# Per-subject residual matmul: the first trip round the ring of x is loaded by SP, and each store waits for a later load

## The chip, the cores and the metric

One core of one Trainium2 chip. The metric is the device time of one execution in microseconds (us). The kernel before takes 327.24 us, the median of three runs (326.29 to 327.82). All rows below are of one profiled execution, which took 326.55 us with a span of 324.0 us.

## The reference

For each of 128 samples, a [128, 1024] block of f32 is multiplied by the 128 x 128 weight matrix of its subject and added to itself:

```
w = weights[subjects]                        # weights [8, 128, 128], subjects [128]
out = x + einsum('bct,bcd->bdt', x, w)       # x, out [128, 128, 1024] f32
```

x is 64 MiB and out is 64 MiB.

## The kernel before, in words

The residual costs no pass of its own: an identity is added to the weights, so that one matmul gives x + x*w. A *tile* is two samples, a *pair* is two tiles (four samples, 2 MiB of x and 2 MiB of out). There are 64 tiles, 32 pairs.

- **Loads of x.** `x_ring` has 10 slots for tiles, that is 5 places for pairs. One DMA loads one pair, in pieces of 8 KB. GpSimd (POOL) issues all 32 loads (L133), so they all run on queue q0. It issues pairs 0 to 3 at the start, then before each further load it copies the pair's four weight matrices out of `weight_bank` into `weight_ring` (L150). Pair p from 5 on waits until TensorE has multiplied pair p - 5, which frees its place. Each of the 5 places has a semaphore `x_in`, which a load raises by 16, one from each DMA engine. Pair 4 waits for the landing of pair 0.
- **Matmuls (PE, L235).** 16 weight loads and 16 matmuls for a tile, into one of two PSUM products. The loop `Fori(0, LAPS)` runs 6 laps of 10 tiles, and 4 tiles are written out behind it. Six warm-up matmuls stand ahead.
- **Copies out of PSUM.** A tile has 8 blocks of 32 x 1024; ACT copies 4 or 5 of them (L221), DVE the rest (L199), into `results`, a ring of 6 pairs.
- **Stores.** SP issues one DMA for a pair, in pieces of 16 KB, on queue q1, where the load of the weights (L103) was the first. Ahead of the store of pair p it waits for the copies of pair p and then, at L112, for the landing of pair p + 4 (`X_FIRST`). Stores 28 to 31 have no such wait. The copies of pair p wait for the store of pair p - 6.

The order of work is thus set by the order of instructions on each engine and by semaphores; there is no planner. Each DMA of x or out runs on all 16 DMA engines; a DMA engine that has work on both queues shares its time between them.

Of the kernel before, what the change touches and what calls it, by code (L numbers as in the profile page):

```python
# [6 lines left out]
DMA_INC = 16  # L7
SLOTS = 10
PAIR = 2
LOADS_AHEAD = 4  # L10
PRODUCTS = 2
RESULTS = 6
WARM_UP = 6
X_FIRST = 4


def subject_residual_kernel(nc, x, subjects, weights, out):
# [11 lines left out]
    f32, i32 = mybir.dt.float32, mybir.dt.int32  # L29
    B, C, T = x.shape  # L30
    S, _, D = weights.shape
    assert C == D == nc.NUM_PARTITIONS
    R, Q = 2, 4
    H, K = C // R, D // Q
    TILES = B // 2
    LAPS, REST = divmod(TILES, SLOTS)
    assert LAPS and SLOTS % PRODUCTS == 0 and REST % PRODUCTS == 0
    PAIRS, PAIR_SLOTS = TILES // PAIR, SLOTS // PAIR
    assert SLOTS % PAIR == 0 and REST % PAIR == 0 and LOADS_AHEAD == X_FIRST == PAIR_SLOTS - 1 and PAIR * 2 * K == C
    BANKS = T // PSUM_BANK_COLS  # L40

    SUBJECT_ROWS = 16
# [8 lines left out]
    x_of_pair = x.rearrange("(n j a) (h r) t -> n (a h) j (r t)", j=PAIR, a=2, r=R)  # L51
    out_of_pair = out.rearrange("(n g) (k q) t -> n (g k) (q t)", g=PAIR * 2, q=Q)

    with ExitStack() as ctx:  # L54
        x_ring = ctx.enter_context(nc.sbuf_tensor("x_ring", [C, SLOTS, R, T], f32))
# [19 lines left out]
        bank_low = ctx.enter_context(nc.semaphore("bank_low"))  # L75
        bank_high = ctx.enter_context(nc.semaphore("bank_high"))

        x_in = [ctx.enter_context(nc.semaphore(f"x_in{s}")) for s in range(PAIR_SLOTS)]

        pair_out = [ctx.enter_context(nc.semaphore(f"pair_out{s}")) for s in range(RESULTS)]  # L80
# [20 lines left out]
        @block.sync  # L101
        def _(sp):
            sp.dma_start(weight_halves[:, :, :, :],  # L103
                         weights.rearrange("(i a) (h r) d -> (a h) i (r d)", a=2, r=R)).then_inc(weights_in, DMA_INC)
            for pair in range(PAIRS):
                place = pair % RESULTS
                sp.wait_ge(act_copied, (pair + 1) * PAIR + PRODUCTS)
                sp.wait_ge(dve_copied, (pair + 1) * PAIR + PRODUCTS)

                ahead = pair + X_FIRST  # L110
                if ahead < PAIRS:
                    sp.wait_ge(x_in[ahead % PAIR_SLOTS], (ahead // PAIR_SLOTS + 1) * DMA_INC)  # L112
                sp.dma_start(out_of_pair[pair], results[:, place, :, :]).then_inc(pair_out[place], DMA_INC)
            for place in range(RESULTS):
                sp.wait_ge(pair_out[place], DMA_INC * len(range(place, PAIRS, RESULTS)))

        @block.gpsimd
        def _(pool):
            def subjects_of(pair):

                _, numbers = nc.values_load_multi_w_load_instructions(
                    subject_row[0:1, pair * PAIR * 2:(pair + 2) * PAIR * 2], engines=(mybir.EngineType.Pool,), min_val=0,
                    max_val=S - 1, skip_runtime_bounds_check_because="DVE has clamped subject_row to 0 .. S - 1")
                return numbers

            pool.memset(eye[:, :], 0.0).then_inc(eye_zero, 1)  # L126
            pool.wait_ge(eye_zero, 1)
            for half in (LOW, HIGH):
                pool.affine_select(eye[half, :], eye[half, :], pattern=[[-1, H]], base=0, channel_multiplier=1,  # L129
                                   compare_op=mybir.AluOpType.not_equal, fill=1.0).then_inc(eye_made, 1)  # L130
            def load(pair):
                place = pair % PAIR_SLOTS
                pool.dma_start(x_ring[:, place * PAIR:(place + 1) * PAIR, :, :], x_of_pair[pair]).then_inc(x_in[place], DMA_INC)  # L133

            for pair in range(LOADS_AHEAD):
                load(pair)
            pool.wait_ge(clamped, 1)
            for pair in range(PAIRS):
                if pair % 2 == 0:
                    numbers = subjects_of(pair)  # L140
                if pair == 0:
                    pool.wait_ge(bank_low, 1)
                    pool.wait_ge(bank_high, 2)
                elif pair >= PAIR_SLOTS:

                    pool.wait_ge(multiplied, (pair - PAIR_SLOTS + 1) * PAIR)
                for j in range(PAIR):
                    slot = pair * PAIR % SLOTS + j
                    for a, half in enumerate((LOW, HIGH)):
                        done = pool.tensor_copy(weight_ring[half, slot, :, :],  # L150
                                                weight_bank[half, bass.ds(numbers[(pair % 2 * PAIR + j) * 2 + a], 1), :, :])
                    done.then_inc(picked, 1)
                if pair >= LOADS_AHEAD:

                    pool.wait_ge(picked, (pair + 1) * PAIR)
                    if pair == LOADS_AHEAD:
                        pool.wait_ge(x_in[0], DMA_INC)
                    load(pair)

        @block.vector  # L160
        def _(dve):
# [61 lines left out]

        @block.tensor
        def _(pe):
            def multiply(tile, slot, landed):
                pe.wait_ge(dve_copied, tile + 1)
                pe.wait_ge(act_copied, tile + 1)
                if slot % PAIR == 0:
                    pe.wait_ge(x_in[slot // PAIR], landed)  # L230
                for n in range(BANKS):
                    cols = slice(n * PSUM_BANK_COLS, (n + 1) * PSUM_BANK_COLS)
                    for r in range(R):
                        for a, half in enumerate((LOW, HIGH)):
                            last = pe.matmul(product[slot % PRODUCTS][a][:, cols], weight_ring[half, slot, r, :],  # L235
                                             x_ring[half, slot, r, cols], start=r == 0, stop=r == R - 1,
                                             tile_position=(a * H, 0))
                last.then_inc(multiplied, 1)


            pe.wait_ge(zeroed, 1)
            zeros = results[:, RESULTS - 1, 0, 0:PSUM_BANK_COLS]
            for _ in range(WARM_UP):
                pe.matmul(product[PRODUCTS - 1][0][:, 0:PSUM_BANK_COLS], zeros[:, 0:D], zeros, start=True, stop=True)  # L244
            pe.wait_ge(picked, 1)
            with pe.Fori(0, LAPS) as lap:
                for slot in range(SLOTS):
                    multiply(lap * SLOTS + slot, slot, lap * DMA_INC + DMA_INC)
            for slot in range(REST):
                multiply(LAPS * SLOTS + slot, slot, DMA_INC * (LAPS + 1))  # L250


# [12 lines left out]
```

## Time and profile before

| | us |
|---|---|
| median of three runs | 327.24 |
| profiled execution | 326.55 |
| its span | 324.0 |
| DVE busy | 286.9 (89%) |
| ACT busy | 285.0 (88%) |
| PE busy | 248.8 (77%) |
| POOL busy | 74.3 (23%) |
| DMA queue q0 (loads of x), share of 16 engines' span | 49.5% |
| DMA queue q1 (weights and stores), the same | 49.1% |

The shares of the two queues are shares of the same 16 DMA engines' time, so they add up. The chain that ended last is given by the page as DVE 33%, DMA 26%, PE 26%; it follows single releases, and doesn't say how long an engine could have been late without harm.

### The profile page before, as it was taken

What the parts mean: (1) busy time and instruction counts of PE and PEld (TensorE: products, weight loads), DVE (VectorE), ACT (ScalarE), POOL (GpSimd) and SP (SyncE); (2) the same over time, 40 slices, a digit from 0 to 9 for tenths busy, and PEclk for the clock granted to TensorE, in tenths of its full rate; (3) what the DMA queues carried; (4) which work ended last, traced back from release to release, by engine and by line L of the source; (5) the groups of instructions that cost most, each with busy time, mean ns of one, the idle gap of its engine ahead of it and who ended that gap; (6) DMA issues with size and microseconds to landing.
All of it is one profiled execution on the core that took longest, in us unless ns stands there. A gap on an engine that the chain in (4) does not pass through costs nothing.

```text
span 324.0 us, 3210 instructions
## 1 busy us (share of the span) xinstructions
PE 248.8 (77%) x1036; PEld 104.9 (32%) x1036; DVE 286.9 (89%) x238; ACT 285.0 (88%) x283; POOL 74.3 (23%) x167
## 2 busy tenths in 40 slices
PE   8778778878888887788788888689678887768800
PEld 3323323333333333333333333234233333223300
DVE  4299999999999999999999999999589999986960
ACT  4199999999999999999999999989689998996950
POOL 4752222122222222212222222121221120000000
PEclk9999999999999999999999999999699999998965
DMA  6999999999999999999999999999999999998996
GB/s 213 419 427 422 408 432 424 428 428 431 433 433 425 421 432 427 434 428 431 424 426 434 429 421 437 419 430 429 426 439 421 430 434 423 437 415 342 419 441 281
DMA packets 13880, 134.84 MB, mean 416 GB/s; under 512 B 1056, under 2 KB 1584, under 8 KB 1584
## 3 DMA queue, kind: packets, MB, share of 16 engines
q0 software_dynamic: 8704, 67.11, 49.5%
q1 hardware_dynamic: 5136, 67.64, 49.1%
q8 instruction: 2, 0.03, 0.0%
q14 instruction: 6, 0.05, 0.0%
q10 hardware_dynamic: 32, 0.01, 0.0%
HBM read 67.64 MB, written 67.11 MB: 416 GB/s over the span
## 4 chain that ended last, share of the span: by engine, by line
DVE 33%; DMA 26%; PE 26%; issue 7%; ACT 4%; POOL 1%; DVEq 0%; POOLq 0%
DVE results L199 33%; DMA x_ring<-x 26%; PE product L235 26%; ACT results L221 4%; POOL weight_ring L150 1%; DVEq L54 0%; POOL eye L129 0%; POOLq L150 0%; POOL eye L126 0%; POOLq L129 0%; POOLq L257 0%
## 5 line engine op out<-in xcount | busy, mean ns | idle before, releaser
L221 ACT COPY results<-product 32x1024 f32<-32x1024 f32 x281 | 281.7, 1002 | 23.2 <-PE product L235 18.6
L199 DVE COPY results<-product 32x1024 f32<-32x1024 f32 x231 | 282.2, 1222 | 22.1 <-PE product L235 16.6
L235 PE MATMUL product<-x_ring,weight_ring 64*128 64x512 f32 x1024 | 240.6, 610 | 58.1 <-DVE results L199 40.0
L235 PEld LDWEIGHTS product<-x_ring,weight_ring 64*128 64x128 f32 x1024 | 101.6, 190 | 197.1 <-issue 114.6
L150 POOL COPY weight_ring<-weight_bank 64x256 f32 x128 | 50.5, 395 | 178.3 <-PE product L235 169.0
L133 POOL DMA_DIRECT2D x_ring<-x x32 | 22.9, 717 | 8.4 <-POOL weight_ring L150 8.3
L244 PE MATMUL product<-results 128*128 128x512 f32 x12 | 8.2, 853 | 1.5 <-DVE results L173 1.5
L244 PEld LDWEIGHTS product<-results 128*128 128x128 f32 x12 | 3.3, 285 | 5.5 <-issue 4.1
L205 ACT COPY weight_bank<-weight_halves 64x1024 f32<-64x1024 f32 x1 | 2.0, 2034 | 3.1 <-DVE weight_halves L164 3.1
L169 DVE COPY weight_bank<-weight_halves 64x1024 f32<-64x1024 f32 x3 | 3.2, 1075 | 0.1
L205 ACT ACT_TABLE_LOAD x1 | 1.3, 1283 | 1.3 <-PEq L257 1.3
L177 DVE TENSOR_SCALAR subject_row<-subject_row 1x128 int32<-1x128 int32 x1 | 0.2, 215 | 2.4 <-DMA subject_row<-subjects 2.4
L164 DVE TENSOR_TENSOR weight_halves<-weight_halves,eye 128x256 f32<-128x256 f32 x2 | 0.8, 423 | 0.8 <-DMA weight_halves<-weights 0.8
L173 DVE MEMSET results<- 128x512 f32 x1 | 0.5, 485 | 0.9 <-PEq L257 0.9
L129 POOL TENSOR_SCALAR_AFFINE_SELECT eye<-eye 64x64 f32<-64x64 f32 x2 | 0.5, 232 | 0.3 <-POOL eye L126 0.2
L126 POOL MEMSET eye<- 128x64 f32 x1 | 0.2, 152 | 0.3 <-POOLq L257 0.3
L257 POOL MEMSET const-float32-0.0<- 128x1 f32 x1 | 0.1, 93 | 0.3 <-issue 0.3
L257 POOL MEMSET const-float32-1.0<- 128x1 f32 x1 | 0.1, 93 | 0.0
L257 POOL MEMSET const-uint8-127<- 128x1 uint8 x1 | 0.1, 93 | 0.0
L257 POOL MEMSET const-bfloat16-1.0<- 128x1 bf16 x1 | 0.1, 92 | 0.0
## 6 DMA issues: line engine op xcount, KB each, us to landing
x_ring<-x POOLq DMA_DIRECT2D x32, 2048.0 KB, 28.0
out<-results SPq DMA_DIRECT2D x32, 2048.0 KB, 11.7
weight_halves<-weights SPq DMA_DIRECT2D x1, 512.0 KB, 4.1
subject_row<-subjects ACTq DMA_DIRECT2D x1, 8.0 KB, 3.1
```

The costliest lines, as they stand in the source:

```text
L129: pool.affine_select(eye[half, :], eye[half, :], pattern=[[-1, H]], base=0, channel_multiplier=1, compare_op=mybir.AluOpType.not_equal, fi ...
L133: pool.dma_start(x_ring[:, place * PAIR:(place + 1) * PAIR, :, :], x_of_pair[pair]).then_inc(x_in[place], DMA_INC)
L150: done = pool.tensor_copy(weight_ring[half, slot, :, :], weight_bank[half, bass.ds(numbers[(pair % 2 * PAIR + j) * 2 + a], 1), :, :])
L164: return dve.tensor_tensor(cells, cells, eye[:, :].rearrange("h (s k) -> h s k", s=1).broadcast_to((C, S // 2, H)), add)
L169: return dve.tensor_copy(weight_bank[half, subjects_of, :, :].rearrange("h i r (q k) -> h i r q k", q=Q), weight_halves[source, :, :, :].r ...
L173: dve.memset(results[:, RESULTS - 1, 0, 0:PSUM_BANK_COLS], 0.0).then_inc(zeroed, 1)
L199: last = dve.tensor_copy(target(tile, a, q), rows(tile, a, q))
L205: return act.copy(weight_bank[half, subjects_of, :, :].rearrange("h i r (q k) -> h i r q k", q=Q), weight_halves[source, :, :, :].rearrang ...
L221: last = act.copy(target(tile, a, q), rows(tile, a, q))
L235: last = pe.matmul(product[slot % PRODUCTS][a][:, cols], weight_ring[half, slot, r, :], x_ring[half, slot, r, cols], start=r == 0, stop=r ...
L244: pe.matmul(product[PRODUCTS - 1][0][:, 0:PSUM_BANK_COLS], zeros[:, 0:D], zeros, start=True, stop=True)
L257: nc = bacc.Bacc("TRN2", target_bir_lowering=False, num_devices=1)
```

## The change

SP issues the first five loads of x, pairs 0 to 4, directly behind the load of the weights, on queue q1, with a semaphore of their own for each place (`x_first`); the fifth waits for the landing of the first. POOL issues pairs 5 to 31 only, so `x_in` counts from there. A store of pair p waits for pair p + 5 where it waited for pair p + 4, and stores 26 to 31 have no such wait (before: 28 to 31), so that nothing at SP waits for the last load, pair 31. TensorE's first 10 tiles are written out, waiting on `x_first`; the loop runs 5 laps instead of 6, and the 4 tiles behind it stay. Sizes, pieces and copies are as before.

```diff
--- before.py
+++ after.py
@@ -11,7 +11,6 @@
 PRODUCTS = 2
 RESULTS = 6
 WARM_UP = 6
-X_FIRST = 4
 
 
 def subject_residual_kernel(nc, x, subjects, weights, out):
@@ -36,7 +35,7 @@
     LAPS, REST = divmod(TILES, SLOTS)
     assert LAPS and SLOTS % PRODUCTS == 0 and REST % PRODUCTS == 0
     PAIRS, PAIR_SLOTS = TILES // PAIR, SLOTS // PAIR
-    assert SLOTS % PAIR == 0 and REST % PAIR == 0 and LOADS_AHEAD == X_FIRST == PAIR_SLOTS - 1 and PAIR * 2 * K == C
+    assert SLOTS % PAIR == 0 and REST % PAIR == 0 and LOADS_AHEAD < PAIR_SLOTS and PAIR * 2 * K == C
     BANKS = T // PSUM_BANK_COLS
 
     SUBJECT_ROWS = 16
@@ -75,6 +74,7 @@
         bank_low = ctx.enter_context(nc.semaphore("bank_low"))
         bank_high = ctx.enter_context(nc.semaphore("bank_high"))
 
+        x_first = [ctx.enter_context(nc.semaphore(f"x_first{s}")) for s in range(PAIR_SLOTS)]
         x_in = [ctx.enter_context(nc.semaphore(f"x_in{s}")) for s in range(PAIR_SLOTS)]
 
         pair_out = [ctx.enter_context(nc.semaphore(f"pair_out{s}")) for s in range(RESULTS)]
@@ -102,14 +102,19 @@
         def _(sp):
             sp.dma_start(weight_halves[:, :, :, :],
                          weights.rearrange("(i a) (h r) d -> (a h) i (r d)", a=2, r=R)).then_inc(weights_in, DMA_INC)
+            for place in range(PAIR_SLOTS):
+                if place >= LOADS_AHEAD:
+                    sp.wait_ge(x_first[place - LOADS_AHEAD], DMA_INC)
+                sp.dma_start(x_ring[:, place * PAIR:(place + 1) * PAIR, :, :], x_of_pair[place]).then_inc(x_first[place], DMA_INC)
             for pair in range(PAIRS):
                 place = pair % RESULTS
                 sp.wait_ge(act_copied, (pair + 1) * PAIR + PRODUCTS)
                 sp.wait_ge(dve_copied, (pair + 1) * PAIR + PRODUCTS)
 
-                ahead = pair + X_FIRST
-                if ahead < PAIRS:
-                    sp.wait_ge(x_in[ahead % PAIR_SLOTS], (ahead // PAIR_SLOTS + 1) * DMA_INC)
+
+                ahead = pair + PAIR_SLOTS
+                if ahead < PAIRS - 1:
+                    sp.wait_ge(x_in[ahead % PAIR_SLOTS], ahead // PAIR_SLOTS * DMA_INC)
                 sp.dma_start(out_of_pair[pair], results[:, place, :, :]).then_inc(pair_out[place], DMA_INC)
             for place in range(RESULTS):
                 sp.wait_ge(pair_out[place], DMA_INC * len(range(place, PAIRS, RESULTS)))
@@ -128,12 +133,6 @@
             for half in (LOW, HIGH):
                 pool.affine_select(eye[half, :], eye[half, :], pattern=[[-1, H]], base=0, channel_multiplier=1,
                                    compare_op=mybir.AluOpType.not_equal, fill=1.0).then_inc(eye_made, 1)
-            def load(pair):
-                place = pair % PAIR_SLOTS
-                pool.dma_start(x_ring[:, place * PAIR:(place + 1) * PAIR, :, :], x_of_pair[pair]).then_inc(x_in[place], DMA_INC)
-
-            for pair in range(LOADS_AHEAD):
-                load(pair)
             pool.wait_ge(clamped, 1)
             for pair in range(PAIRS):
                 if pair % 2 == 0:
@@ -150,12 +149,11 @@
                         done = pool.tensor_copy(weight_ring[half, slot, :, :],
                                                 weight_bank[half, bass.ds(numbers[(pair % 2 * PAIR + j) * 2 + a], 1), :, :])
                     done.then_inc(picked, 1)
-                if pair >= LOADS_AHEAD:
+                if pair >= PAIR_SLOTS:
 
                     pool.wait_ge(picked, (pair + 1) * PAIR)
-                    if pair == LOADS_AHEAD:
-                        pool.wait_ge(x_in[0], DMA_INC)
-                    load(pair)
+                    place = pair % PAIR_SLOTS
+                    pool.dma_start(x_ring[:, place * PAIR:(place + 1) * PAIR, :, :], x_of_pair[pair]).then_inc(x_in[place], DMA_INC)
 
         @block.vector
         def _(dve):
@@ -223,11 +221,11 @@
 
         @block.tensor
         def _(pe):
-            def multiply(tile, slot, landed):
+            def multiply(tile, slot, landed, turns):
                 pe.wait_ge(dve_copied, tile + 1)
                 pe.wait_ge(act_copied, tile + 1)
                 if slot % PAIR == 0:
-                    pe.wait_ge(x_in[slot // PAIR], landed)
+                    pe.wait_ge(landed[slot // PAIR], turns)
                 for n in range(BANKS):
                     cols = slice(n * PSUM_BANK_COLS, (n + 1) * PSUM_BANK_COLS)
                     for r in range(R):
@@ -243,11 +241,13 @@
             for _ in range(WARM_UP):
                 pe.matmul(product[PRODUCTS - 1][0][:, 0:PSUM_BANK_COLS], zeros[:, 0:D], zeros, start=True, stop=True)
             pe.wait_ge(picked, 1)
-            with pe.Fori(0, LAPS) as lap:
+            for slot in range(SLOTS):
+                multiply(slot, slot, x_first, DMA_INC)
+            with pe.Fori(0, LAPS - 1) as lap:
                 for slot in range(SLOTS):
-                    multiply(lap * SLOTS + slot, slot, lap * DMA_INC + DMA_INC)
+                    multiply(lap * SLOTS + SLOTS + slot, slot, x_in, lap * DMA_INC + DMA_INC)
             for slot in range(REST):
-                multiply(LAPS * SLOTS + slot, slot, DMA_INC * (LAPS + 1))
+                multiply(LAPS * SLOTS + slot, slot, x_in, DMA_INC * LAPS)
 
 
 def kernel(x, itok_B_0_7, L0_cond_weights):
```

## Rows read from the trace of the kernel before

**Rows 1.** The page, part 2, 40 slices: DMA engines' mean busy share in tenths, and GB/s.

```profile
DMA  6999999999999999999999999999999999998996
GB/s 213 419 427 422 408 432 424 428 428 431 433 433 425 421 432 427 434 428 431 424 426 434 429 421 437 419 430 429 426 439 421 430 434 423 437 415 342 419 441 281
```

**Rows 2.** The page, part 3, DMA queues: packets, MB, share of 16 engines' span.

```profile
q0 software_dynamic: 8704, 67.11, 49.5%
q1 hardware_dynamic: 5136, 67.64, 49.1%
q8 instruction: 2, 0.03, 0.0%
```

**Rows 3.** Waits of SP's queue, whole span: us in total, times, longest.

```profile
SPq L112 <- DMA x_ring<-x: 271.9, 27, 30.6
```

**Rows 4.** Windows of the start: stretch, its us, PE, PEld, DVE, ACT, POOL busy, PEclk, DMA share, GB/s.

```profile
4.00:5.00 1.00, 1.00 (x2) 0.34 (x1) 0.18 (x2) 0.00 (x0) 0.71 (x2) 1.00 0.51 185
5.00:6.00 1.00, 1.00 (x3) 0.45 (x2) 0.97 (x3) 0.34 (x1) 0.00 (x0) 1.00 0.94 262
6.00:8.00 2.00, 2.00 (x5) 0.94 (x4) 1.96 (x3) 1.70 (x1) 0.00 (x0) 1.00 0.98 369
8.00:12.00 4.00, 2.06 (x6) 0.68 (x6) 0.93 (x1) 0.00 (x0) 2.50 (x7) 1.00 1.01 416
12.00:30.00 18.00, 14.90 (x68) 6.19 (x66) 14.43 (x12) 13.90 (x14) 9.19 (x22) 1.00 1.01 425
```

**Rows 5.** Timeline of the start: start us, us, engine, line, operation.

```profile
0.74 0.43 SPq L103 DMA_DIRECT2D weight_halves<-weights  x1
...
1.75 2.96 POOL L133 DMA_DIRECT2D x_ring<-x  x4
...
21.12 0.71 POOL L133 DMA_DIRECT2D x_ring<-x  x1 [0.30 <-POOL weight_ring L150]
...
38.34 0.33 PEld L235 LDWEIGHTS product<-x_ring,weight_ring 64*128 64x128 f32 x4 [1.46 <-DVE results L199]
```

**Rows 6.** Line L133, the first four loads: us from issue to landing.

```profile
DMA to landing us min/median/max: 9.8/16.2/22.8
```

**Rows 7.** Chain that ended last: start us, us, what.

```profile
47.68 3.73 PE product L235 x16
...
251.61 37.48 DMA x_ring<-x
...
289.23 5.42 PE product L235 x16
```

**Rows 8.** DMA queues in 39 to 42 us, while both queues have work.

```profile
q1 hardware_dynamic: 53, 0.87, 67.5%
q0 software_dynamic: 51, 0.42, 32.8%
```

**Rows 9.** DMA queues in 291.5 to 295.2 us.

```profile
q1 hardware_dynamic: 94, 1.38, 87.2%
q0 software_dynamic: 6, 0.05, 3.2%
```

**Rows 10.** DMA queues in 295.6 to 296.7 us.

```profile
q1 hardware_dynamic: 4, 0.03, 7.2%
```

**Rows 11.** SP's timeline about 295.5 and about 313 us: its store issues.

```profile
295.95 0.33 SPq L113 DMA_DIRECT2D out<-results  x1
...
313.36 0.33 SPq L113 DMA_DIRECT2D out<-results  x1
```

**Rows 12.** Line L113, all stores: us from issue to landing.

```profile
DMA to landing us min/median/max: 8.0/11.7/17.1
```

**Rows 13.** Windows of the end, columns as in group 4.

```profile
295.20:295.60 0.40, 0.40 (x4) 0.22 (x2) 0.40 (x1) 0.40 (x1) 0.00 (x0) 1.00 0.20 82
...
302.50:304.50 2.00, 0.84 (x4) 0.01 (x2) 1.99 (x2) 1.38 (x3) 0.00 (x0) 1.00 0.95 393
...
321.60:323.00 1.40, 0.00 (x0) 0.00 (x0) 0.00 (x0) 0.00 (x0) 0.00 (x0) 0.50 0.11 47
```

## The prediction, on record before the kernel ran

> **What bounds the kernel now.** I read first the strip of 40 slices: the DMA engines stand at 9 tenths in 37 of them and move 408 to 441 GB/s, with low ends at the first slice (213), the 37th (342) and the last (281) [rows 1]. Then the queues: q0 and q1 take 49.5% and 49.1% of the same 16 engines' time, 98.6% together [rows 2]. So the kernel is bound by the time of the DMA engines, although DVE and ACT are busy 89% and 88%. A look at SP says how the two kinds of transfer are ordered: it waits 271.9 us for loads of x, in 27 of its waits [rows 3], so stores are nearly always held back for a load, but rarely with an idle DMA engine. The load issued at 251.61 lands 37.48 us later [rows 7], while a load alone takes (4.0 + 22.8 - 1.75 - 9.8) / 3 = 5.1 us (first to last of the four issues at the start, which lie in a stretch of 2.96 us from 1.75 that puts the last at about 4.0 [rows 5, 6]): there are several loads in the queue ahead of it, and q0 doesn't run dry before the last one. The bytes don't change, so the end can move only by time in which the DMA engine that ends last is idle or slow.
>
> **Where such time is.** (a) At the start. In 4 to 5 us the DMA share is 0.51 and in 5 to 6 us 0.94; the rate is 262, 369 and 416 GB/s in 5 to 6, 6 to 8 and 8 to 12 us against 425 after that [rows 4]. Lost: 0.49 + (1 - 262/425) + 2 x (1 - 369/425) + 4 x (1 - 416/425) = 0.49 + 0.38 + 0.26 + 0.08 = 1.2 us, of which 0.49 + 0.06 = 0.55 us idle. (b) At the last load. In 295.6 to 296.7 us the engines are at 7.2% of 16, which is 1.15 of an engine [rows 10], and in the 0.4 us before at 0.20 [rows 13]; store 27, which waits for load 31, is issued at 295.95 [rows 11]. That is a hole of some 1.5 us. (c) At the end: in 321.6 to 323.0 us 0.11 of 16, so two engines still work when fourteen are done [rows 13].
>
> (b) and (c) belong together. In 291.5 to 295.2 us q0 has 3.2% of 16, half an engine [rows 9]: fourteen or fifteen engines have long finished load 31, one has not, and it shares its time with a store. This late engine works on through the hole (the 1.15), and its own end sets the end of the span. So the hole costs the other engines time, but not the end.
>
> **The change part by part.**
>
> *Loads 0 to 4 from SP.* Five DMA issues are added to SP behind one of 0.43 us at 0.74, so the first is issued at about 1.2 instead of 1.75 [rows 5], and it stands in the weights' own queue: each DMA engine goes on to x where its weights end. That gives back the idle 0.55 us of (a). The slow 0.66 us that remain may be due to POOL's descriptors (gone now) or to the first touches of memory (not gone); I take 0.25 of them. Sum -0.8 us. Bounds: -1.2, and +0.3 if pieces of 8 KB from SP's queue start later than POOL's did, for which no row stands. POOL saves 2.96 us [rows 5], beside its wait for the weight bank: nothing. SP's wait for load 0 before load 4 holds the SP queue until about 11 us, and behind it stand only stores, the first of which left after load 4 before, so after 26.8 (4.0 + 22.8): nothing.
>
> *Order of loads 3 to 5.* Load 5 leaves POOL at about 21.1 as before [rows 5], but on q0 while loads 3 and 4 are on q1. Pieces are equal (8 KB), so each queue gets half. From 22 load 3 has about 4 of its 5.1 us left, so it lands at 30 instead of 26.8; load 4 then shares with load 5 and load 6 and lands by 40. PE takes up pair 3 at 38.34 [rows 5] and pair 4 at 47.68 [rows 7], so both have over 7 us of cover: nothing. If the cover were gone, PE would still have the backlog of DMA work behind it to hide it in.
>
> *Stores wait one load further.* One transfer of 4.9 us (2.1 MB at 428) goes from stores before to loads before; the sum is the same. New cost can only come by the ring of results: copies of pair p need store p - 6, which now leaves at the landing of load p - 1 and takes 11.7 us [rows 12]. A pair's load and store together take 9.8 us (4.2 MB at 428 GB/s, the middle of [rows 1]), so loads land so far apart and the store is in 1.9 us after load p, and the first copy of the pair that began at 289.23 came 5.42 us after [rows 7]. Cover 3.5 us; without it ACT and DVE would be late, then POOL's next load, which stands several loads ahead: nothing at the end.
>
> *None waits for the last load.* Closes hole (b) for the fourteen or fifteen engines, worth 0 at the end by the argument above, 1.5 us if that argument is wrong. The next thing late is the late engine itself.
>
> *Fewer loads of POOL's kind.* The late engine is 1.5 us behind in (b) and 1.5 more in (c), 3.0 in all. If its lag comes with POOL's loads, 5 of 32 of them gone takes off 0.5; if not, 0. I take -0.2. The Trainium skill (DMA: Bandwidth & Descriptors, Latency and other measured facts) says that DMA engines 7 and 15 are usually slower, by its best guess through the rings of GpSimd's descriptors, and that sync's queue has no such rings; by it the term would be -0.5 and the sum -1.0. The trace agrees that one or two engines are late, but doesn't say why.
>
> *Ten tiles written out on PE.* Each has 16 weight loads and 16 matmuls, so 320 instructions more. The trace has two packets of instructions on q8, 0.03 MB together [rows 2], for 14 written tiles; with 24 a third is likely. Such a packet holds up one DMA engine. Its cost: in 302.5 to 304.5 us, where a dip has no other cause in view, the share is 0.95 [rows 13] against the 1.01 of full stretches [rows 4], that is 0.06 x 2 x 16 = 1.9 us of one engine; the least is 0, when it falls on an engine that isn't last. The second late engine in (c), absent in (b), fits this. I take +0.3, near the low end, since a packet in the middle of the run hits an engine that by (b) isn't the late one. The Trainium skill (Runtime: NRT & Kernel Launch, Instruction fetch mechanics) says that instructions come in blocks of 16 KiB, 256 of them: 320 more cross one border and perhaps two, and the term would be up to +1.9 by it; two packets of 0.03 MB together agree with the size.
>
> **Sum.** -0.8 - 0.2 + 0.3 = -0.7 us: the span goes from 324.0 to 323.3, the profiled execution from 326.55 to 325.85. The median is 0.7 above the profiled execution, so the forecast is 327.24 - 0.7 = 326.5.
>
> **The rivals.**
> 1. *The hole counts.* If the late engine isn't the same in (b) and (c), or was idle in the hole after all, the end moves by the hole as well: -1.5 - 1.2 = -2.7, 324.5. For it: the packets of a window aren't named by engine. Against: 1.15 engines at work throughout, and two at the end. Chance 0.2.
> 2. *The block of instructions falls on the late engine.* +1.9 - 0.8 - 0.2 = +0.9, 328.1. Chance 0.12.
> 3. *The change doesn't do what it says at the start*, since SP's queue pays the same slow start: 0, 327.2. Chance 0.11.
> 4. *The last load starves (slower).* Stores 25 to 29 are now released together at the landing of load 30, and against them a load gets a third of an engine: 32.8% to 67.5% [rows 8]. Load 30 lands at 289.1 now; with one store fewer ahead of it and the earlier start at 289.1 - 4.9 - 0.8 = 283.4. Load 31 runs alone for about 1 us, then has 4 us left at a third, 12 us: 296.4. Store 31 left 313.36 - 295.95 = 17.4 us after load 31 [rows 11] and needs at least 8.0 to land [rows 12]: 321.8, under the forecast end of 323.3. Past 297.9 for load 31 this chain decides. If load 30 isn't earlier, load 31 lands at 302.1, the end is at 327.5 and the span, 0.4 more, at 327.9: +3.9, 331.1. Against: the late engine profits too from a store less. Chance 0.07.
>
> **How the numbers follow.** The forecast, -0.2 to -1.4, has 0.5. My own range is 325.8 to 327.1; since the three runs shown lie within 1.5 us of each other, and rivals 1 and 2 hold a third, I take 324.9 to 328.1. What a measurement can tell from no change is about 0.5%, 1.6 us. Faster than 325.6: rival 1 nearly whole and the forecast's edge, 0.23. Slower than 328.9: rival 4 and a bit of rival 2, 0.08. The rest, 0.69, within 0.5%.
>
> **What would show it.** In the windows of 4 to 6 us a DMA share near 1; the first load landed by 10.7 instead of 11.55 (1.75 + 9.8). Among the DMA issues 27 loads from POOL and 5 from SP. No window of 1 us near 285 to 300 with a share under 0.5. At the end again a window of 1 to 3 us (longer than before, since the other engines gain the hole) with 0.06 to 0.13 of 16: that is the step on which most hangs. If all engines end together, 2 us or more earlier, rival 1 was right. Three packets on q8. Store 31 issued before 315; after that, rival 4. The prediction is wrong if a window in the middle has a DMA share under 0.9, which would be a backlog that ran dry.

## The result, and the profile after

The changed kernel takes 323.91 us, the median of six runs (323.70 to 324.13), against 327.36 (326.23 to 327.82) before: a ratio of 0.9903, 95% interval 0.9884 to 0.9922. The forecast was 326.5 with a range from 324.9: the direction was right, the size four to five times too small, and the time lies under the range. In the longer series of the experiments (17 to 29 runs each) the kernel before had medians of 326.6 to 326.8; against those the change is worth 2.8 us, and that is the size used below. The profiled execution took 324.13 us with a span of 322.1 (before 326.55 and 324.0).

The page after, parts 2 and 3 (40 slices of DMA share and of GB/s; queues with packets, MB, share of 16 engines):

```profile
DMA  7999999999999999999999999999999999999994
GB/s 280 423 423 421 428 441 409 431 424 428 429 426 435 425 432 419 426 441 418 432 435 427 417 430 432 426 422 437 419 429 434 426 430 422 440 426 431 429 429 208
...
q1 hardware_dynamic: 6496, 78.12, 57.2%
q0 software_dynamic: 7344, 56.62, 41.8%
q8 instruction: 3, 0.05, 0.1%
```

Against [rows 1, 2]: the first slice carries 280 GB/s where it was 213, the dip of 342 in the 37th slice is gone, and the last slice has less, 208 where it was 281. Five loads have moved from q0 to q1, and q8 has three packets of instructions instead of two.

A packet counts in the window in which it begins, which is why a share can pass 1. The start, windows with the columns of [rows 4], then SP's issues and the first matmul of x in the timeline, then the time to landing of SP's five loads:

```profile
4.00:5.00 1.00, 1.00 (x2) 0.34 (x1) 0.17 (x1) 0.00 (x0) 0.00 (x0) 1.00 1.06 436
5.00:6.00 1.00, 1.00 (x3) 0.50 (x2) 0.97 (x3) 0.37 (x1) 0.00 (x0) 1.00 1.13 475
6.00:8.00 2.00, 2.00 (x6) 0.95 (x5) 1.96 (x3) 1.67 (x1) 0.00 (x0) 1.00 0.98 414
8.00:12.00 4.00, 2.71 (x12) 1.03 (x12) 0.90 (x1) 0.00 (x0) 2.56 (x7) 1.00 1.01 424
```

```profile
1.24 8.93 SPq L108 DMA_DIRECT2D x_ring<-x  x5
...
10.03 2.42 PE L233 MATMUL product<-x_ring,weight_ring 64*128 64x512 f32 x10 [1.29 <-POOL weight_ring L149]
```

```profile
DMA to landing us min/median/max: 8.5/17.4/25.7
```

There is no window with idle engines, and none with a low rate either: 414 to 475 GB/s where before stood 185, 262, 369 and 416 [rows 4]. The first load is issued at 1.24 and lands 8.5 us later, at 9.8 (before 1.75 + 9.8 = 11.55 [rows 5, 6]).

SP's waits for loads, its last store, and the end in windows:

```profile
SPq L117 <- DMA x_ring<-x: 259.5, 26, 24.7
```

```profile
309.07 0.33 SPq L118 DMA_DIRECT2D out<-results  x1
```

```profile
290.00:292.00 2.00, 0.00 (x0) 0.00 (x0) 1.99 (x2) 1.98 (x3) 0.00 (x0) 0.99 0.99 426
...
317.00:318.00 1.00, 0.00 (x0) 0.00 (x0) 0.00 (x0) 0.00 (x0) 0.00 (x0) 0.50 0.50 213
318.00:319.00 1.00, 0.00 (x0) 0.00 (x0) 0.00 (x0) 0.00 (x0) 0.00 (x0) 0.50 0.27 115
319.00:321.00 2.00, 0.00 (x0) 0.00 (x0) 0.00 (x0) 0.00 (x0) 0.00 (x0) 0.50 0.06 25
```

Stores wait for loads nearly as long as before (259.5 us; 271.9 in [rows 3]), but no engine is idle about the last load: 0.99 in 290 to 292 us. Store 31 leaves at 309.07 instead of 313.36 [rows 11]. At the end half of the engines' time is used in 317 to 318, a quarter in 318 to 319, and 0.06 of 16, one engine, in 319 to 321. That is the late engine of the prediction, now alone for some two us.

### The profile page after: what moved, and what is told of

Read it like the earlier page. It is cut to its first block, busy times and chain, and to the rows that moved or that the text cites. A ratio compares the mean times of both kernels' runs of the same rounds, so it can differ in the third digit from the quotient of the medians.

```text
span 322.1 us, 3197 instructions
## 1 busy us (share of the span) xinstructions
PE 246.1 (76%) x1036; PEld 103.6 (32%) x1036; DVE 286.9 (89%) x238; ACT 285.3 (89%) x283; POOL 71.2 (22%) x162
## 4 chain that ended last, share of the span: by engine, by line
DVE 39%; PE 27%; DMA 13%; ACT 9%; issue 7%; POOL 1%; ACTq 0%; POOLq 0%
DVE results L197 37%; PE product L233 27%; DMA x_ring<-x 11%; ACT results L219 9%; DMA weight_halves<-weights 1%; DVE weight_bank L167 1%; POOL weight_ring L149 1%; ACTq L53 0%; DVE weight_halves L162 0%; POOLq L149 0%; POOLq L126 0%; POOLq L142 0%
## 5 line engine op out<-in xcount | busy, mean ns | idle before, releaser
L156 POOL DMA_DIRECT2D x_ring<-x x27 | 19.4, 720 | 8.0 <-POOL weight_ring L149 8.0
L242 PE MATMUL product<-results 128*128 128x512 f32 x12 | 7.3, 772 | 1.5 <-DVE results L171 1.5
```

## The experiments

Each was timed beside the kernel before, whose medians were so close (326.56 to 326.76) that the times are compared with one another as they are.

**1. The new start without the new store waits.** The changed kernel with

```diff
-                ahead = pair + PAIR_SLOTS
-                if ahead < PAIRS - 1:
+                ahead = pair + PAIR_SLOTS - 1
+                if ahead < PAIR_SLOTS:
+                    sp.wait_ge(x_first[ahead], DMA_INC)
+                elif ahead < PAIRS:
```

> The changed kernel with the store waits of before (store p waits for load p + 4, store 27 for the last load, 31); SP's first loads and the ten written-out tiles stay. Theory A (the start was mis-sized, the DMA engine that ends last sets the end): the first load landed at 9.79 us in the changed kernel against 11.53, so 1.7 to 1.8 us of the gain are here: 327.4 - 1.8 = 325.6, ratio 0.9945. Theory B (the hole before store 27 counts): the same 1.8 here, and 1.5 more only when that wait goes, so 325.6 here too; it is the next two kernels that tell them apart. Theory C (the start is hidden again later): 327.4.

Measured: 323.94 us (323.72 to 324.82), ratio 0.9913 (0.9898 to 0.9928). All of the gain is here, and more than the 1.8 that theories A and B gave it (theory C gave nothing).

**2. The new store waits alone**, in the kernel before (`ahead = pair + PAIR_SLOTS`, `if ahead < PAIRS - 1`).

> The kernel before with only the store waits changed: store p waits for load p + 5, none waits for load 31. Loads stay with POOL, TensorE's code is unchanged. Theory A: the hole in 295 to 297 us goes, the late DMA engine still ends last: 327.4, ratio 1.000, and at the end a longer stretch in which one or two engines work alone (3 us). Theory B: the end moves by the hole, 1.5 us: 325.9, ratio 0.9955.

Measured: 327.02 us, ratio 1.0016 (0.9993 to 1.0039). Theory A's number. Two windows of it, about 36 us and at the end:

```profile
36.00:40.00 4.00, 3.60 (x16) 1.35 (x16) 3.89 (x4) 3.95 (x5) 0.21 (x1) 1.00 1.01 346
...
322.70:324.40 1.70, 0.00 (x0) 0.00 (x0) 0.00 (x0) 0.00 (x0) 0.00 (x0) 0.50 0.05 19
```

A single engine works in 322.7 to 324.4. And in 36 to 40 us the engines are busy (1.01) at 346 GB/s: their packets are *stretched*, that is, each takes longer than usual for the same bytes. This is a loss that the share of busy time doesn't show.

**3. Only the wait of store 27 for the last load taken away**, in the kernel before (`if ahead < PAIRS - 1`, distance 4 kept).

> The kernel before with one wait taken away: store 27 doesn't wait for the last load (31); all other stores wait for load p + 4 as before. Theory A: no change, 327.4. Theory B: -1.5, 325.9. If gate_only gains and this doesn't, it is the one transfer of further waiting that gains, not the hole.

Measured: 325.69 us, ratio 0.9971 (0.9958 to 0.9983), -1.0 us. Theory A's number (no change) was wrong here, and theory B's -1.5 too large: the hole is worth two thirds of its length. Against experiment 2, waiting one load further costs 1.3 us beside it. The slow spell that experiment 2 has in 36 to 40 us isn't in this profile:

```profile
36.00:40.00 4.00, 3.44 (x16) 1.19 (x14) 3.89 (x4) 3.96 (x4) 0.38 (x1) 1.00 1.01 428
```

**4. TensorE's first ten tiles written out, alone** (loop of 5 laps behind them).

> The kernel before with only TensorE's first ten tiles written out (loop of 5 laps behind them). Theory A and B: three packets of instructions on q8 where there were two; +0.3 us by the prediction, 0 to +1.9 by its bounds: 327.7, ratio 1.001.

Measured: 326.43 us, ratio 0.9985 (0.9966 to 1.0003): no cost that shows, with a third packet on q8 in its trace.

**5. The first five loads back at POOL, all else as changed.** SP's five loads are taken out, and at POOL stands (cut at the dots)

```diff
+            def first(place):
+                pool.dma_start(x_ring[:, place * PAIR:(place + 1) * PAIR, :, :], x_of_pair[place]).then_inc(x_first[place], DMA_INC)
+
+            for place in range(0, LOADS_AHEAD):
+                first(place)
...
+                if pair == LOADS_AHEAD:
+                    pool.wait_ge(picked, (pair + 1) * PAIR)
+                    pool.wait_ge(x_first[0], DMA_INC)
+                    first(pair)
```

> The changed kernel with the first five loads issued by POOL again (on x_first, load 4 behind the landing of load 0); the new store waits and the ten written-out tiles stay. Theory A (who issues the first loads is the whole gain; it is idle time, stretched packets of POOL's queue at the start, and a second such spell near 34 to 56 us): 323.9 + 2.8 = 326.7, the first load lands at 11.5 to 12.0 us. Theory B (the gain is in the waits and the written-out code): stays at 324 to 325.

Measured: 326.69 us (325.57 to 328.15), ratio 1.0009 (0.9989 to 1.0028). Undoing this one part undoes the whole gain, 2.8 us, and brings back runs 2.6 us apart. Its start in windows:

```profile
4.00:5.00 1.00, 1.00 (x2) 0.34 (x1) 0.30 (x2) 0.00 (x0) 0.71 (x2) 1.00 0.86 265
...
6.00:8.00 2.00, 2.00 (x5) 0.92 (x4) 1.96 (x3) 1.57 (x1) 0.00 (x0) 1.00 0.97 315
```

In 6 to 8 us the engines are busy 0.97 and carry 315 GB/s, where the changed kernel has 0.98 and 414. A second slow spell stands much later, in 60 to 75 us; here is this kernel's window and, under it, the changed kernel's:

```profile
60.00:75.00 15.00, 12.18 (x54) 4.87 (x54) 14.59 (x13) 14.68 (x16) 2.58 (x6) 1.00 1.00 383
60.00:75.00 15.00, 12.83 (x59) 5.49 (x57) 14.73 (x13) 14.70 (x16) 4.34 (x10) 1.00 0.99 419
```

The late spell costs about 1.3 us by my estimate, 15 x (419 - 383) / 428 (428 GB/s is the middle of [rows 1]): in this profile about as much of the loss lies there as at the start.

**6. SP issues load 0 alone**, POOL loads 1 to 3 at the start and load 4 behind the landing of load 0.

> As the kernel before this one, but load 0 alone is issued by SP, loads 1 to 4 by POOL at the start. If POOL's packets are stretched because POOL's queue is young in the first 10 us, load 0 lands at 9.5 to 9.8 only if SP's packets aren't slowed by POOL's beside them; loads 0 and 1 share the engines, so load 0 would land later (13 to 14) and load 1 beside it. Theory A1 (the stretched packets belong to POOL's queue at the start, whatever else runs): about half of the gain, 325.3, with an excess of packet time on q0 in 4 to 10 us. Theory A2 (only the idle gap between the weights and the first x counts): all of the gain, 324.0 to 324.5.

Measured: 327.76 us, ratio 1.0035 (1.0022 to 1.0049), slower than either. Neither number was met. Load 0 landed at 13.4 us, sharing the engines with load 1 from the other queue, as expected; what wasn't foreseen is a hole in 33 to 36, 1.6 us by the share of 0.48. Windows, and what was issued at that time:

```profile
33.00:36.00 3.00, 3.00 (x16) 1.47 (x15) 2.97 (x3) 2.96 (x4) 2.07 (x5) 1.00 0.48 194
36.00:40.00 4.00, 2.92 (x16) 1.21 (x14) 3.94 (x4) 3.94 (x5) 0.00 (x0) 1.00 0.96 338
```

```profile
34.80 0.71 POOL L162 DMA_DIRECT2D x_ring<-x  x1 [0.30 <-POOL weight_ring L151]
35.01 0.36 SPq L115 DMA_DIRECT2D out<-results  x1
```

Both queues had run dry: load 6 waited for pair 1, which was late because load 0 was, and store 0 waited for load 5. Behind the hole 36 to 40 us runs at 338 GB/s with a share of 0.96: stretched packets again.

**7. One queue.** All loads from SP, the load of pair p + 5 ahead of the store of pair p. The wait of a store for a load and POOL's loads are gone; added is

```diff
+                ahead = pair + PAIR_SLOTS
+                if ahead < PAIRS:
+                    slots = ahead % PAIR_SLOTS
+                    sp.wait_ge(picked, (ahead + 1) * PAIR)
+                    sp.dma_start(x_ring[:, slots * PAIR:(slots + 1) * PAIR, :, :], x_of_pair[ahead]).then_inc(x_in[slots], DMA_INC)
                 sp.wait_ge(act_copied, (pair + 1) * PAIR + PRODUCTS)
```

> The changed kernel with all 32 loads of x issued by SP on q1, load p + 5 ahead of the store of pair p; no wait of a store for a load is left, and POOL issues none. If the engine that ends last is late because of POOL's loads, all 16 engines end within 0.6 us of each other (1.9 and 4.3 us before and after the change), and the time is 322.0 or less. If its lag has another cause (instruction fetches), the lag stays and the time is 323.5 to 324.5. Rival: with one queue the loads stand behind the stores and compute is late at some point: a window with a DMA share under 0.9, and slower than 325.

Measured: 324.65 us (324.55 to 324.72), ratio 0.9938 (0.9917 to 0.9959), 0.7 us over the changed kernel and just over the 323.5 to 324.5 expected if the lag stays. q1's row of the page, and the end:

```profile
q1 hardware_dynamic: 13840, 134.75, 98.8%
```

```profile
318.00:320.00 2.00, 0.00 (x0) 0.00 (x0) 0.00 (x0) 0.00 (x0) 0.00 (x0) 0.50 0.23 98
320.00:321.20 1.20, 0.00 (x0) 0.00 (x0) 0.00 (x0) 0.00 (x0) 0.00 (x0) 0.50 0.06 27
```

With no load from POOL at all, three to four engines work in 318 to 320 and one in 320 to 321.2. So the late engine isn't made by POOL's loads. Why the kernel is 0.7 us slower wasn't tried.

**8. Loads 5 to 31 from ACT**, behind its copies of pair p - 5.

> The changed kernel with loads 5 to 31 issued by ACT, behind its copies of pair p - 5, instead of by POOL: two hardware queues. By the first theory of the kernel before this one the lag of the last engine goes as well: 322.0 or less. ACT pays an issue for each pair, 27 x 0.4 us, beside copies of 8.9 us a pair against 9.8 us of DMA time a pair: no cost while it stays under that. Rival: ACT becomes the bound, slower than 325.

Measured: 323.76 us (323.66 to 323.95), ratio 0.9911 (0.9890 to 0.9932): the changed kernel's time, with one engine late again. It says the same as 7.

**9. Loads 0 to 3 from ACT's own hardware queue**, load 4 from SP behind the landing of load 0.

> The changed kernel with loads 0 to 3 issued by ACT on its own hardware queue (q10), load 4 by SP. Theory H (a hardware queue is what gains, wherever it stands): 324 us, first load landed by about 10. Theory W (what gains is that x stands behind the weights in their own queue, so that the weights aren't disturbed and no engine idles): x and weights now share the engines, the weights land later than 4.8 us, and part of the gain is lost: 325 or more.

Measured: 324.14 us (323.96 to 324.32), ratio 0.9919 (0.9894 to 0.9943). Theory H's number: x needn't stand behind the weights in one queue.

**10 and 11. More fetches of instructions, and fewer.** TensorE's loop written out whole; and the copies of ACT and DVE in loops.

```diff
-            with pe.Fori(0, LAPS - 1) as lap:
+            for lap in range(LAPS - 1):
```

```diff
+            with act.Fori(0, ROUNDS - 1) as turn:
+                for tile in range(ROUND):
+                    copy_tile(tile, turn * ROUND + (ROUND + tile + 1), turn * DMA_INC + DMA_INC if tile % PAIR == 0 else None)
```

> The changed kernel with TensorE's loop of 5 laps written out: no loop at all, some 2000 instructions, so 8 or 9 packets of 16 KB on q8 instead of 3. Theory F (each fetch of instructions puts one DMA engine back by 0.6 to 1.7 us, and the engine that ends last sets the end): slower than the changed kernel by 1 to 3 us, 325 to 327, with more engines late in the last 5 us. Theory S (the lag is a slow engine, whatever is fetched): 323.9.

> The changed kernel with the copies of ACT and DVE in loops of 12 tiles (a first round of 12 written out, 4 turns, 4 tiles behind; ACT takes 53 of 96 blocks of a round instead of 52.8): fewer instructions, so fewer packets on q14. Theory F: the engines that end last gain 0.6 us for each fetch saved on them: 0.5 to 1.5 us faster than the changed kernel, 322.4 to 323.4. Theory S: 323.9. Rival: register work and the turn of the loop make DVE late, slower than 324.2.

Measured: 323.91 us for the first (one of six runs at 325.60), 323.85 for the second; ratios 0.9922 (0.9893 to 0.9952) and 0.9910 (0.9886 to 0.9935). The queue rows of the two:

```profile
q8 instruction: 8, 0.13, 0.2%
```

```profile
q14 instruction: 4, 0.03, 0.0%
```

Eight packets of 16 KB in place of three cost nothing, two of 8 KB fewer (4, before 6) gave nothing. Theory F falls for the time of the kernel.

**12. The wait for the last load put back into the changed kernel** (`if ahead < PAIRS`, distance 5).

> The changed kernel with the wait of a store for the last load back (store 26 waits for load 31). If the hole is worth what it was in the kernel before, 324.9. If in the changed kernel an engine that works through the hole sets the end, 323.9. With the store waits of before the time was 323.94, so I expect 323.9 to 324.2.

Measured: 325.41 us, ratio 0.9960 (0.9941 to 0.9979), +1.5. My own expectation (323.9 to 324.2) missed. The hole and the end:

```profile
288.00:290.00 2.00, 1.66 (x8) 1.00 (x10) 1.99 (x2) 1.96 (x3) 0.00 (x0) 1.00 0.36 147
290.00:292.00 2.00, 2.00 (x10) 0.67 (x6) 1.97 (x3) 1.98 (x3) 0.00 (x0) 1.00 0.03 12
...
293.00:322.40 29.40, 7.18 (x32) 2.69 (x30) 13.19 (x11) 12.32 (x13) 0.00 (x0) 0.72 0.99 419
322.40:323.30 0.90, 0.00 (x0) 0.00 (x0) 0.00 (x0) 0.00 (x0) 0.00 (x0) 0.50 0.01 0
```

With the further wait the hole is longer, and in 290 to 292 us even the late engine is nearly idle (0.03 of 16, half an engine). It catches up: the share is 0.99 up to 322.4 and then 0.01, so all sixteen stop at nearly the same time. In experiment 1, with the distance of 4, the emptiest half microsecond of the hole still had one engine at work (in a profiled run that was the slowest of its six, 324.82), and there the hole cost nothing that shows (323.94, and 323.79 without it in experiment 14):

```profile
295.00:295.50 0.50, 0.50 (x4) 0.00 (x1) 0.50 (x1) 0.49 (x2) 0.00 (x0) 1.00 0.08 33
```

**13. POOL's first load issued earlier**, ahead of its work on the identity; the kernel before otherwise.

```diff
+            for pair in range(1):
+                load(pair)
             pool.memset(eye[:, :], 0.0).then_inc(eye_zero, 1)
...
-            for pair in range(LOADS_AHEAD):
+            for pair in range(1, LOADS_AHEAD):
                 load(pair)
```

> The kernel before with POOL's first load of x ahead of its work on the identity, so issued at about 0.75 us instead of 1.75; loads 1 to 3 stay behind that work. If the late issue is the cause, the first load lands at about 10 and the time falls by 1.5 to 2.8 us, to 324 to 325.3. If it is POOL's queue at the start (its packets are slow there, whenever they were issued), the first load lands at 11 or later and the time stays above 326.

Measured: 325.15 us (324.84 to 325.40), ratio 0.9957 (0.9941 to 0.9973). The issue, its landing (the first is the shortest), and two windows:

```profile
1.27 0.83 POOL L128 DMA_DIRECT2D x_ring<-x  x1 [0.82 <-POOLq L259]
```

```profile
DMA to landing us min/median/max: 8.3/27.2/40.2
```

```profile
4.00:5.00 1.00, 1.00 (x2) 0.34 (x1) 0.35 (x2) 0.00 (x0) 1.00 (x2) 1.00 1.07 441
...
6.00:8.00 2.00, 2.00 (x6) 0.92 (x5) 1.96 (x3) 1.48 (x1) 0.00 (x0) 1.00 1.02 430
```

The issue moved by only half a microsecond, from 1.75 to 1.27. The first load lands at 1.27 + 8.3 = 9.6, 2 us earlier; 4 to 5 us has no idle engine, 6 to 8 us carries 430 GB/s instead of 369, and the runs lie within 0.6 us. At the start POOL's queue is as good as SP's if it isn't late; the time, 325.15, is still 1.2 above experiment 1, which has the same waits of stores.

**14. The new start, the old distance of 4, no wait for the last load.**

> The changed kernel with the store of pair p waiting for load p + 4 again, and none for the last load: the new start and the closed hole without the further wait. If the parts measured in the kernel before add up here (+1.3 for the further wait, -1.0 for the hole), 322.6 to 322.9. If a DMA engine that ends at 321.4 to 321.6 of the span in all kernels with SP's start sets the end, 323.7 to 324.0, as in the changed kernel.

Measured: 323.79 us (323.50 to 324.00), ratio 0.9912 (0.9888 to 0.9935). The parts don't add up; the second expectation held.

**15. SP late.** The changed kernel with `sp.wait_ge(subjects_in, DMA_INC)` ahead of SP's first load of x.

> The changed kernel with SP waiting for the landing of the subject numbers (2.2 to 3.8 us) before its first load of x, so x starts at about 4.5 to 5 us and the DMA engines idle for some 0.5 us behind the weights, as with POOL's late issue. Gap theory (a pause there is followed by stretched packets, from any queue): first load at 11 to 12 us, 325.7 to 326.5, and runs more than 1 us apart. Queue theory (only POOL's late packets are stretched): the idle time alone is lost, first load at 10.0 to 10.6, 324.4 to 324.7, runs within 0.5 us.

Measured: 325.60 us (324.98 to 326.23), ratio 0.9971 (0.9957 to 0.9984), 0.1 under the gap theory's range and 1.7 over the changed kernel, with runs 1.25 us apart. Landing, the start in windows, the queue in 4.4 to 5.0 us and, under it, the changed kernel's in 4.5 to 5.0 us, and 36 to 40 us:

```profile
DMA to landing us min/median/max: 7.6/16.6/24.2
```

```profile
4.00:5.00 1.00, 1.00 (x2) 0.34 (x1) 0.50 (x2) 0.00 (x0) 0.00 (x0) 1.00 0.91 133
4.20:4.40 0.20, 0.20 (x2) 0.20 (x1) 0.00 (x0) 0.00 (x0) 0.00 (x0) 1.00 0.00 0
5.00:6.00 1.00, 1.00 (x4) 0.49 (x3) 0.97 (x2) 0.71 (x1) 0.00 (x0) 1.00 0.75 229
6.00:8.00 2.00, 2.00 (x6) 0.92 (x5) 1.96 (x3) 1.33 (x1) 0.00 (x0) 1.00 1.01 426
```

```profile
q1 hardware_dynamic: 16, 0.13, 150.3%
q1 hardware_dynamic: 20, 0.16, 77.2%
```

```profile
36.00:40.00 4.00, 3.32 (x16) 1.30 (x15) 3.89 (x4) 3.94 (x5) 0.79 (x2) 1.00 1.02 360
```

Issued at 3.40, the first load lands at 3.40 + 7.6 = 11.0. No packet begins in 4.2 to 4.4 us: that is the pause. The 16 packets of 8 KB that begin behind it, by 5.0 us, take 1.503 x 0.6 = 0.90 us each; in the changed kernel one takes 0.772 x 0.5 x 16 / 20 = 0.31. The rate in 5 to 6 us is 229 GB/s at a share of 0.75. From SP the spell is over by 6 us (426 at 1.01), while with POOL's late issue the rate in 6 to 8 us is still 369 [rows 4] or 315 (experiment 5). A second slow spell stands in 36 to 40 us, 360 GB/s at 1.02, on a kernel that has none when SP isn't late. So it is the pause, not the queue, for 1.7 of the 2.8 us.

**16. Experiment 13 without the wait of store 27 for the last load.**

> The kernel of e13 (POOL's first load 1 us earlier, otherwise the kernel before) with no wait of store 27 for the last load. If the hole is worth there what it was in the kernel before (1.0 us), 325.15 - 1.0 = 324.2. If the DMA engine that ends last works through the hole, 325.15.

Measured: 324.56 us (324.35 to 324.76), ratio 0.9941 (0.9919 to 0.9962): -0.6, between the two theories.

## Why the prediction was wrong

*The bound was right.* The kernel is bound by the DMA engines' time; in the changed one store 31 left at 309.07, 13 us ahead of the end of the span (322.1), and stood behind other stores.

*Loads 0 to 4 from SP: the step that failed.* The term was -0.8 us with a lower bound of -1.2; it measures -2.8 (experiment 5 against the changed kernel; experiment 1 gives the same). I had counted the idle 0.55 us and a part of the low rate in 5 to 12 us, and took the stretch as a fact of POOL's descriptors or of first touches that would mostly stay. The runs show three things in its place. First, idle engines and stretched packets come and go together: the engines run out of work between the weights and x, and the packets behind that pause are slow, from SP's queue too (experiment 15); without the pause both are gone, from POOL's queue too (experiment 13). That makes the first load 1.8 us earlier in the profiles, at 9.8 where the prediction allowed 10.7. Second, kernels with the pause can have another slow spell later, in 36 to 40 us in experiments 2 and 15 and in 60 to 75 us in experiment 5 (experiment 3 has none in 36 to 40); I had summed windows up to 12 us only. With both gone, the spread of the runs is too (2.6 us in experiment 5, 0.4 in the changed kernel). Third, 0.5 us lies outside the span, below. The pause, at 1.6 to 1.7 us (experiments 13 and 15), and this 0.5 make 2.1 to 2.2 of the 2.8; no experiment isolates the remaining 0.6 to 0.7. What I should have asked of [rows 4] is why the engines were busy 0.98 in 6 to 8 us and carried only 369 GB/s: a full share at a low rate is lost time, and what ends it isn't bounded by the windows where it is seen.

*None waits for the last load: half right.* The sign on which most hung came: an engine alone in the last two us. "Worth 0 at the end" held with the new start and the distance of 4 (323.94 with the hole, 323.79 without it), where an engine works through the hole. It failed in the kernel before (-1.0) and with POOL's earlier start (-0.6), although the profile of before shows the same picture. One profiled execution shows which engine was last in it; the runs of that kernel lie 1.6 us apart, and in others it may be an engine that idled in the hole. That is argued, not shown.

*Stores wait one load further: wrong at nothing.* It costs 1.3 us in the kernel before (experiment 2 against 3) but nothing with the new start (323.91 against 323.79, experiment 14), so that cost goes with the pause: of the two profiles only that of experiment 2 has the slow spell in 36 to 40 us. That the further wait brings the spell isn't shown. And it makes the hole at the last load longer: with it the hole costs 1.5 us (experiment 12). The change takes away the wait for the last load in the same edit. In the kernel before, the two cancel (+1.3 and -1.0, together 1.0016), and in the changed kernel the sum is again nothing (323.91 against 323.94).

*The order of loads 3 to 5: right*; no hole came of it. Experiment 6 shows that the cover has an end: with load 0 late by 3.6 us both queues ran dry at 33 to 36.

*Fewer loads of POOL's kind: wrong.* I took -0.2. With none of them the late engine stayed (experiments 7 and 8). The Trainium skill's best guess for slow engines, the rings of GpSimd's descriptors (DMA: Bandwidth & Descriptors, Latency and other measured facts), isn't borne out by the lag seen here.

*Ten tiles written out: cost too high.* A third packet came, as predicted, but +0.3 is 0 within the measurement, and eight packets cost no more.

*The rivals.* Rival 1 had the time nearest to the result, 324.5, but not the reason: the hole gives nothing in the changed kernel beyond what the further wait costs. Rival 2, a block of instructions on the late engine, and rival 3, SP's queue paying the same slow start, were both wrong: the third packet cost nothing that shows, and 4 to 5 us carries 436 GB/s. Rival 4, starvation of the last load, didn't show: store 31 left at 309.07.

*What stays open:* why packets are stretched behind the pause at the start and behind the hole of experiment 6 but not behind the hole at the last load, what brings the later slow spell, and why one engine ends 2 us after nearly all others. The trace names no engine for a packet.

## What to carry to other kernels

Where the DMA engines are the bound, look at the first microseconds for a pause between the first small load and the stream: here issuing POOL's first load half a microsecond earlier was worth 1.6 us (experiment 13), and holding SP's back by 2.2 us cost 1.7 (experiment 15), since the packets behind that pause are slow from either queue. Read share and rate together, since a share of 1 at 80% of the usual rate is a loss like an idle engine. No version beat the changed kernel clearly: experiments 8 (323.76) and 14 (323.79) are the same within the runs.

## What was not expected of the hardware

- Packets behind a pause of all DMA engines can be stretched, on either kind of queue: 133 GB/s at 0.91 from SP's queue (experiment 15, 4 to 5 us), 315 at 0.97 from POOL's (experiment 5, 6 to 8 us), 338 at 0.96 behind the hole of experiment 6, against 420 to 430 elsewhere. A pause alone isn't enough: behind the hole before the last stores nothing of it shows, 419 GB/s at 0.99 in 293 to 322.4 in experiment 12, the usual rate for that share (424 at 1.01 in 8 to 12 us of the changed kernel).
- The time outside the span, profiled execution minus its span, is 2.5 us in all eight kernels in which POOL issues 31 or 32 loads (326.55 - 324.0 before, 327.7 - 325.2 in experiment 6) and 1.8 to 2.2 in all in which it issues 27 or none (324.13 - 322.1 after, 324.55 - 322.6 in experiment 7). The difference, 2.55 against 2.03, makes 0.5 us of the gain; its cause wasn't tried.
- Taking instruction packets away or adding five of 16 KB moved a kernel that is bound by its DMA engines by nothing that can be measured.
